# Attention's stacks turned by transposing DMAs on SP's queue instead of on TensorE

## The chip, the cores and the metric

The kernel runs on one NeuronCore of a Trainium2 chip. The metric is the time on the device of one execution, in microseconds (us). Engines are called PE (TensorE, matrix products; PEld is its weight load), DVE (VectorE), ACT (ScalarE), POOL (GpSimd) and SP (SyncE, which here only issues DMAs). SPq is SP's issuing of DMAs, as the trace shows it.

## What is computed

Two layers over 64 sequences of 64 tokens with 128 channels. Layer 0 is attention with 16 heads of 8 channels over the sequence's own keys and 64 context keys, then a feed-forward block with 8 routed experts and a shared one; layer 1 mixes a de-pooled context into the tokens and adds a two-of-eight expert block. The change touches only layer 0's attention:

```python
qkv = (x @ w_qkv.T).reshape(B, N, 3, H, D)
k = concatenate([extra_k, k]);  v = concatenate([extra_v, v])
attn = softmax(einsum('bhnd,bhmd->bhnm', q * scale, k))
out = einsum('bhnm,bhmd->bhnd', attn, v)
x = x + tanh(g_xattn[0]) * (out @ w_proj.T + b_proj)
```

## The kernel before, in words

The 4096 tokens are 32 tiles of 128 (two sequences each). The attention stage is a software pipeline over tiles that every engine walks by itself: in step k an engine does, in a fixed order written out by hand in its `step`, one piece for tile k, another for tile k-1, and so on; `stage(n)` is the tile n steps back (None outside 0 to 31). Each engine executes strictly in its written order, and semaphores (`S["name"]`) tie the engines together. `walk` peels the first steps and runs the rest in a hardware loop of four steps a turn. The stage ends at about 235 us of the profile; sorting, the routed experts and layer 1 follow and aren't touched.

For one tile t the pieces that matter are:

- ACT, stage 0 (`ctx_hi`, L678) writes the high half of the context keys into `stack[:, t%2, 2]`. PE, stage 1, makes q, k and v (L1492); ACT (L726) writes the fp16 high halves of q and k, each twice, into `stack[:, t%2, 0:2]` and signals `hi_ready`; it then saves v (L728); DVE writes the low halves (L992, `lo_ready`, and L1004 for the context keys, `ctx_stacked`). The stack has two buffers, by the tile's parity. Each of its three parts is 128 tokens x 16 heads x 32 fp16.
- PE, stage 2 (`turn_stack`, L1411) turns the three parts, four 128x128 transposes each, into PSUM banks 5 and 6: first q and k (8 transposes), later in the step the context keys (4). ACT copies the turned q to `qc` (L711), DVE the turned own keys to `ktp` (L974), ACT the turned context keys to `ktp` (L718). `qc` and `ktp` have four slots, by t%4.
- PE, stage 3 (`scores_for_max`, L1313, in two halves) computes scores from `qc` and `ktp`, and DVE takes their negative maxima (L935, four a tile). PE, stage 4, turns these (L1432), and ACT copies them to `mT` (L701, `max_kept`).
- SP, stage 3 in its own count, waits for `max_kept` and issues four small DMAs (L427, 1 KB each) that put the maxima into spare rows of `qc`; they signal `shift_placed`.
- PE, stage 5 (`scores_by_key`, L1329, two halves) waits for `shift_placed`, computes the shifted scores; ACT exponentiates them (L685); PE averages the values (`average`, L1342); then come the turn back (L1510), normalising, projection, the residual and the router's work (L1452).

SP's own step in this stage holds nothing but the wait for `max_kept` and the four DMAs. POOL spreads v, does small vector work and, from 107 us on, scatters rows to HBM (L551, indirect DMAs).

Of the kernel before, what the change touches and what calls it, by code (L numbers as in the profile page):

```python
# [102 lines left out]
def flamingo_gated_two_layers(nc, x, ctx_k, ctx_v_swapped, consts, gates, w_qkv, w_proj, b_proj, gate_w,  # L103
                              sh_gate_up, sh_down, rt_gate_up, rt_down, patch_mask, w_in, b_in, g_res, g_init,
                              router_w, router_b, expert_w, expert_b, out):
    NT = x.shape[1] // P
    D = P
    H, HD = 16, 8
# [15 lines left out]
    with ExitStack() as ctx:  # L124
# [179 lines left out]
        def by_seq(bank):  # L304
            return bank.rearrange("p (g b t) -> p b g t", g=G, b=2)

        def bank16(b):
            return PS[:, b, :].bitcast(F16)


        TILE_CHUNKS = [(0, 2), (2, 8), (8, NT)]
        x_in = [sem(f"x_in{c}") for c in range(3)]
        ck_in = [sem(f"ck_in{c}") for c in range(3)]
        cv_in = [sem(f"cv_in{c}") for c in range(3)]
        consts_in = sem("consts_in")
        weights_in = sem("weights_in")
        qkv_in, qkv_ready = sem("qkv_in"), sem("qkv_ready")
# [9 lines left out]
                 "o_kept o_turned recip_ready o_normed on_turned on_kept projected x_updated")  # L327
        S = {n: sem("a_" + n) for n in names.split()}
        shift_placed = [sem("a_shift_placed0"), sem("a_shift_placed1")]

        for n in "stats moments var_eps copied normed kept xnT_done xnT_kept routed".split():
            S["r_" + n] = sem("r_" + n)
# [44 lines left out]
        def arrived(eng, sems, tile):  # L377

            if tile is not None and tile.turn is None:
                for c, (lo, _) in enumerate(TILE_CHUNKS):  # L380
                    if tile.n == lo:
                        eng.wait_ge(sems[c], 16)
                        eng.nop(nofuse=True)

        def zero_tails(eng, half):
# [15 lines left out]
        @block.sync  # L401
        def _(sp):
            sp.dma_start(X[:, 0:2 * D], x[:, 0:2 * D]).then_inc(x_in[0], 16)
            sp.dma_start(cst[:], consts).then_inc(consts_in, 16)
            sp.dma_start(wqkv[:], w_qkv).then_inc(qkv_in, 16)
            sp.dma_start(CK[:, 0:2 * D], ctx_k[:, 0:2 * D]).then_inc(ck_in[0], 16)
            sp.dma_start(gate[:], gates).then_inc(gate_in, 16)
            sp.dma_start(wproj[:], w_proj).then_inc(weights_in, 16)
            sp.dma_start(bproj[:], b_proj).then_inc(weights_in, 16)
            sp.dma_start(gatew[:], gate_w).then_inc(weights_in, 16)  # L410
            sp.dma_start(pm_i[:], patch_mask).then_inc(mask_in, 16)
            for c in range(3):
                lo, hi = TILE_CHUNKS[c]
                if c:
                    sp.dma_start(X[:, lo * D:hi * D], x[:, lo * D:hi * D]).then_inc(x_in[c], 16)
                    sp.dma_start(CK[:, lo * D:hi * D], ctx_k[:, lo * D:hi * D]).then_inc(ck_in[c], 16)
                sp.dma_start(CV[:, lo * D:hi * D], ctx_v_swapped[:, lo * D:hi * D]).then_inc(cv_in[c], 16)
            for dst, src in ((shgu, sh_gate_up),):
                sp.dma_start(dst[:], src).then_inc(more_in, 16)

            def step(stage):
                a = stage(3)
                if a:

                    sp.wait_ge(S["max_kept"], a.done())
                    for hg in range(HG):
                        sp.dma_start(qc[32 * hg + 24:32 * hg + 25, a.slot, :, :],  # L427
                                     mT[HG * hg:HG * hg + G, a.par, :]).then_inc(shift_placed[a.par], 16)

            walk(sp, NT, LAGS, step)  # L430
            zero_tails(sp, 0)
            sp.wait_ge(rows_known, 1)
            sp.wait_ge(spare_zero, 16)
            sp.wait_ge(tails_zero, 16 * E)
            sp.wait_ge(scattered, 16 * NT)

            def load_rows(stage):
                l = stage(0)
                if l:
                    if not (l.turn is None and l.n < 4):  # L440
                        sp.wait_ge(S["e_turned"], l.freed(back=4))
                    row = sp.value_load(rows_of[0:1, ds(l.t, 1)], min_val=0, max_val=ROWS - P)
                    sp.dma_start(xs[:, l.slot, :], sorted_x[ds(row, P)]).then_inc(xs_in[l.slot], 16)

            walk(sp, NS, 2, load_rows)

            def store_out(stage):
                o = stage(12)
                if o:
                    sp.wait_ge(S["l_out_ready"], o.done())  # L450
                    sp.dma_start(out[:, o.cols(D)], X[:, o.cols(D)]).then_inc(out_done, 16)

            walk(sp, NT, 12, store_out)
            sp.wait_ge(out_done, 16 * NT)
# [210 lines left out]
        def _(act):  # L665
# [8 lines left out]

            def ctx_hi(f):
                arrived(act, ck_in, f)
                act.wait_ge(S["ctx_turned"], f.freed())
                nc.scalar.copy(parts(f.par, 2, 8, 0, 16).rearrange("p h (c d) -> p h c d", c=2),  # L678
                               twice_over(CK[:, f.cols(D)].rearrange("p (h d) -> p h d", h=H)))\
                    .then_inc(S["ctx_hi"], 1)  # L680
# [6 lines left out]
            def step(stage):  # L687
# [17 lines left out]
                if f:  # L705
                    act.wait_ge(S["qkv_done"], f.freed())
                    act.wait_ge(S["xnT_done"], f.done())
                    nc.scalar.copy(xnT[:, f.par, :], PS[:, 4, 0:P]).then_inc(S["xnT_kept"], 1)  # L708
                if s:
                    act.wait_ge(S["qk_turned"], s.done())  # L710
                    nc.scalar.copy(qc[:, s.slot], bank16(5)[:, 0:512].rearrange("p (g t) -> p g t", g=G))\  # L711
                        .then_inc(S["q_kept"], 1)
                if b:
                    exp_chunk(b, 2)
                    exp_chunk(b, 3)
                if s:
                    act.wait_ge(S["ctx_turned"], s.done())
                    last = nc.scalar.copy(ctx_half(s.slot), by_seq(bank16(6)[:, 0:512]))  # L718
                    last.then_inc(S["ctx_kept"], 1)
                if f:  # L720
                    act.wait_ge(S["qk_turned"], f.freed())
                    act.wait_ge(S["qkv_done"], f.done())

                    hi = parts(f.par, 0, 0, 8, 16).rearrange("p w h (c d) -> p w h c d", c=2)
                    qk = PS[:, 4, P:3 * P].rearrange("p (w h d) -> p w h d", w=2, h=H)
                    last = nc.scalar.copy(hi, qk.unsqueeze(3).to_broadcast([P, 2, H, 2, HD]))  # L726
                    last.then_inc(S["hi_ready"], 1)
                    nc.scalar.copy(XN2[:, ds(f.t, 1), 0:D], PS[:, 4, 3 * P:4 * P].unsqueeze(1)).then_inc(S["v_kept"], 1)  # L728
# [48 lines left out]
                    shared_gate(3, 0)  # L777
                    shared_gate(3, 1)

            walk(act, NT, 12, step, lambda: act.wait_ge(ck_in[2], 16), drain=gates_in_drain)  # L780
            act.wait_ge(S["h_acted"], Tile(EARLY - 1).done(2, 1))

            def sorted_step(stage):
# [74 lines left out]
        def _(dve):  # L858
# [79 lines left out]
            def step(stage):  # L938
# [28 lines left out]
                if m:  # L967
# [1 line left out]
                    dve.wait_ge(S["r_stats"], m.done())  # L969
                    dve.nop(nofuse=True)  # L970
                    dve.bn_aggr(mv2[:, m.par, :], str_[:, m.par, :]).then_inc(S["r_moments"], 1)  # L971
                if s:
                    dve.wait_ge(S["q_kept"], s.done())
                    last = dve.tensor_copy(own_half(s.slot), by_seq(bank16(5)[:, 512:1024]))  # L974
                    last.then_inc(S["k_kept"], 1)
# [63 lines left out]
                elif k == 12:  # L1039
                    shared_product(1, 1)  # L1040

            walk(dve, NT, 13, step, lambda: dve.wait_ge(x_in[2], 16), drain=products_in_drain)

            chained = [0]

# [246 lines left out]
        def _(pe):  # L1292
# [8 lines left out]

            def scores_for_max(a, half):

                if half == 0:
                    pe.wait_ge(S["q_kept"], a.done())
                    pe.wait_ge(S["k_kept"], a.done())
                    pe.wait_ge(S["ctx_kept"], a.done())
                pe.wait_ge(S["maxed"], a.freed(4, 2 * half + 1, back=2))
                for g in range(G):
                    for b in range(2):  # L1310
# [106 lines left out]
            def step(stage):  # L1417
# [2 lines left out]
                if a:  # L1420
                    scores_for_max(a, 0)

                if a:
                    pe.wait_ge(S["ctx_kept"], a.done())
                if rk:
                    pe.wait_ge(S["r_xnT_kept"], rk.done())
# [6 lines left out]
                                        ident16[:]).then_inc(S["max_turned"], 1)  # L1433
                if b:
                    scores_by_key(b, 0)
                if s:

                    if s.turn is None and s.n == 0:
                        pe.wait_ge(weights_ready, 1)
                    pe.wait_ge(S["hi_ready"], s.done())  # L1440
                    pe.wait_ge(S["lo_ready"], s.done())
                    turn_stack(s, 0, 5, 0, None)
                    turn_stack(s, 1, 5, 512, "qk_turned")
# [53 lines left out]
                    pe.wait_ge(S["k_placed"], ro.quad_done(2, 0))  # L1497
                if m:
                    pe.wait_ge(S["x_updated"], m.done())
                if s:  # L1500
                    pe.wait_ge(S["ctx_stacked"], s.done())
                    turn_stack(s, 2, 6, 0, "ctx_turned")
                if b:
                    average(b, 1)
                if n:
                    pe.wait_ge(S["o_kept"], n.done())
                    if s:
                        pe.wait_ge(S["k_kept"], s.done())
                    for g in range(G):
                        last = nc.tensor.transpose(PS[:, 5, g * P:g * P + P], oS[:, n.par, g * P:g * P + P], identf)  # L1510
                    last.then_inc(S["o_turned"], 1)
                if s:
                    pe.wait_ge(S["ctx_kept"], s.done())
                if rt:
                    pe.wait_ge(S["r_normed"], rt.done())
# [209 lines left out]
```

## Time and profile before

| | |
|---|---|
| median of 3 runs | 506.03 us |
| lowest and highest | 502.38 and 506.38 us |
| the profiled execution's own time | 496.49 us |
| its span in the profile | 494.9 us |
| PE, DVE, ACT, POOL busy | 445.5, 373.7, 288.3, 321.0 us |
| mean granted TensorE clock | 0.983 of full |

The profile is of one execution. A busy share says how long an engine's instructions were in flight; matmuls overlap, so a busy PE isn't PE at its peak. A row of a timeline gives the start, the length until the group's last end, engine, line, operation, written and read tiles, and the count; in brackets, the idle time before it and what ended that. "Issue" of a DMA is the time in which the issuing engine is held; landing is later.

### The profile page before, as it was taken

To read this page: it belongs to the slowest core of one execution; us is meant where nothing else is said; L and a number is where in the kernel's file an instruction comes from. 1 tells how busy PE (TensorE), PEld (TensorE's weight loads), DVE (VectorE), ACT (ScalarE), POOL (GpSimd) and SP (SyncE) were. 2 spreads that over 40 slices of the span, in tenths; PEclk is the share of its full clock that TensorE was granted. 3 is DMA by queue.
4 is the path that set the end of the run, shared out by engine and by line. 5 is a ranking of instruction groups with operands and counts; after the bars stand their busy time and mean duration, and the time that the engine had idled before them with its cause. 6 is when DMAs were issued, how large, how long until landed. Compare 5 with 4: busy or idle time off the path is not lost. (4 is left out here: it accounts for less than half of the span.)

```text
span 494.9 us, 20976 instructions
## 1 busy us (share of the span) xinstructions
PE 445.5 (90%) x6894; PEld 351.8 (71%) x6895; DVE 373.7 (76%) x1197; ACT 288.3 (58%) x803; POOL 321.0 (65%) x783
## 2 busy tenths in 40 slices
PE   1689999999999999987987999987997799999998
PEld 0457777776767777764656988864655699898997
DVE  3577999989888888954678666644766688888984
ACT  1448999999989898875225454434233344344431
POOL 5544775567777777766743665677825888998630
PEclk9999999999999999999899999998999599999999
DMA  7930000000000000000145677741000011111001
GB/s 228 413 140 4 26 26 5 5 10 15 11 12 11 11 11 12 15 15 19 55 148 147 212 222 224 221 139 32 17 11 13 16 40 37 37 39 36 23 23 33
DMA packets 22538, 33.61 MB, mean 68 GB/s; under 512 B 5592, under 2 KB 16656, under 8 KB 21968
## 3 DMA queue, kind: packets, MB, share of 16 engines
q0 software_dynamic: 7552, 20.20, 12.9%
q1 hardware_dynamic: 14352, 12.39, 7.7%
q8 instruction: 34, 0.56, 0.5%
q10 hardware_dynamic: 576, 0.26, 0.2%
q14 instruction: 24, 0.20, 0.1%
HBM read 24.82 MB, written 7.86 MB: 66 GB/s over the span
## 5 line engine op out<-in xcount | busy, mean ns | idle before, releaser
L935 DVE TENSOR_REDUCE negm<-PS 128x4 f16<-128x512 f32 x128 | 82.0, 682 | 1.1 <-PE PS L1313 0.4
L685 ACT ACTIVATE pexp<-PS 128x512 f32<-128x512 f32 x128 | 69.4, 594 | 3.8 <-PE PS L1329 3.1
L1645 PE MATMUL PS<-w,vp 128*128 128x128 f32 x512 | 63.3, 277 | 0.0
L1645 PEld LDWEIGHTS PS<-w,vp 128*128 128x128 f32 x512 | 60.5, 194 | 0.0
L1342 PE MATMUL PS<-pexp,vp 128*32 128x64 f32 x2048 | 49.4, 226 | 0.2
L1539 PE MATMUL PS<-xsT,wst 128*128 128x128 f32 x320 | 44.5, 282 | 3.5 <-DMA wst<-in_rt_gate_up_dram 1.3
L1539 PEld LDWEIGHTS PS<-xsT,wst 128*128 128x128 f32 x320 | 38.8, 191 | 8.2 <-issue 6.8
L1342 PEld LDWEIGHTS PS<-pexp,vp 128*32 128x32 f32 x2048 | 33.7, 111 | 13.8 <-issue 8.2
L551 POOL DMA_INDIRECT sorted_x<-VALL,posu x32 | 32.9, 1027 | 14.0 <-issue 7.3
L1266 DVE TENSOR_TENSOR vp<-PS,xnT 128x1024 f32<-128x1024 f32 x32 | 38.7, 1208 | 0.8 <-PE PS L1622 0.8
L1411 PEld LDWEIGHTS PS<-ident,stack 128*128 128x128 f16 x384 | 26.2, 103 | 17.9 <-issue 12.7
L580 POOL DMA_DIRECT2D wst<-in_rt_gate_up_dram x40 | 21.5, 539 | 26.6 <-PE PS L1539 18.9
L610 POOL DMA_INDIRECT VALL<-sorted_y,places x32 | 32.4, 1014 | 7.4 <-issue 7.0
L1411 PE MATMUL PS<-ident,stack 128*128 128x128 f16 x384 | 34.8, 231 | 2.0 <-DVE stack L992 2.0
L1173 DVE TENSOR_TENSOR stack<-PS,oS 128x256 f32<-128x256 f32 x40 | 16.9, 423 | 23.8 <-ACT oS L792 23.8
L852 ACT CAST mask1T<-PS 96x128 bf16<-96x128 f16 x32 | 8.4, 261 | 44.7 <-PE PS L1654 44.3
L792 ACT ACTIVATE oS<-PS 128x256 f32<-128x256 f32 x40 | 15.3, 384 | 31.7 <-PE PS L1539 31.3
L1492 PE MATMUL PS<-wqkv,xnT 128*128 128x384 f32 x64 | 32.9, 598 | 0.9 <-ACT xnT L708 0.9
L1313 PE MATMUL PS<-ktp,qc 32*64 32x128 f16 x1024 | 28.2, 230 | 4.2 <-ACT ktp L718 2.7
L492 POOL TENSOR_TENSOR ve<-mv,epsc 128x1 f32<-128x1 f32 x32 | 6.0, 188 | 39.7 <-DVE mv L971 39.5
L1553 PE MATMUL PS<-rdn,stack 128*128 x160 | 25.4, 281 | 3.6 <-DVE stack L1173 2.8
L583 POOL DMA_DIRECT2D sorted_y<-YS x40 | 21.8, 546 | 9.7 <-DVE YS L1169 4.8
(240 smaller groups left out, 1265.4 us busy)
## 6 DMA issues: line engine op xcount, KB each, us to landing
wst<-in_rt_gate_up_dram POOLq DMA_DIRECT2D x40, 256.0 KB, 3.6
xs<-sorted_x SPq DMA_DIRECT2D x40, 64.0 KB, 2.8
sorted_y<-YS POOLq DMA_DIRECT2D x40, 64.0 KB, 3.1
qc<-mT SPq DMA_DIRECT2D x128, 1.0 KB
out_dram<-X SPq DMA_DIRECT2D x32, 64.0 KB
X<-in_x_dram SPq DMA_DIRECT2D x1, 1536.0 KB, 8.5
CK<-in_ctx_k_dram SPq DMA_DIRECT2D x1, 1536.0 KB, 11.9
CV<-in_ctx_v_swapped_dram SPq DMA_DIRECT2D x1, 1536.0 KB, 17.8
```

Of the source, the lines that this page charges most:

```text
L551: pool.indirect_dma_start(out=sorted_x, out_offset=bass.IndirectOffsetOnAxis(ap=posu[:, o.t:o.t + 1], axis=0), in_=XN2[:, o.t, :], in_offs ...
L610: pool.indirect_dma_start(out=XN2[:, t, 0:D], out_offset=None, in_=sorted_y, in_offset=bass.IndirectOffsetOnAxis(ap=places[:, t:t + 1], ax ...
L685: nc.scalar.activation(pexp[:, j, :], PS[:, 2 + j % 2, :], ACT.Exp).then_inc(S["exped"], 1)
L935: dve.tensor_reduce(negm[:, a.par, :, j], PS[:, j % 2, :].rearrange("p (g k) -> p g k", g=G), AX.X, ALU.max, negate=True).then_inc(S["maxe ...
L1266: dve.tensor_tensor(z[:, m.par], PS[:, 4:6, :].rearrange("p b (e t) -> p (b e) t", t=P), xnT4[:, m.slot, :].unsqueeze(1).to_broadcast([P, ...
L1313: last = nc.tensor.matmul(PS[64 * b:64 * b + 64, hg % 2, g * P:g * P + P], qc[rows, a.slot, g, 64 * b:64 * b + 64], kt[rows, a.slot, b, g, :],
L1342: last = nc.tensor.matmul(PS[32 * g:32 * g + 32, 7, j * P + SEQ * seq:j * P + SEQ * seq + SEQ], vp[:, b.par, seq, g * HG + j, :], pexp[:, ...
L1411: last = nc.tensor.transpose(bank16(bank)[:, col + g * P:col + (g + 1) * P], stack[:, s.par, w, g * HG:g * HG + HG, :].rearrange("p h c -> ...
L1492: nc.tensor.matmul(PS[:, 4, P:4 * P], xnT[:, f.par, :], wqkv[:], start=True, stop=True)\
L1539: last = nc.tensor.matmul(PS[:, 2 + s.par, i * P:i * P + P], wst[:, s.slot, i * P:i * P + P], xsT[:, s.par, :], start=True, stop=True)
L1553: last = nc.tensor.matmul(PS[:, 6 + b.par, 0:D], act2T[:, b.par, i * P:i * P + P], rdn[:, ds(e_down * FF + i * D, D)], start=(i == 0), sto ...
L1645: nc.tensor.matmul(PS[:, 6 + y.par, 0:D], z[:, y.par, e, :], w1[:, e * D:e * D + D], start=(e == 0), stop=False)
```

## The change

From tile 4 on, PE's twelve transposes a tile (L1411) and the three copies (L711, L974, L718) go. In their place SP issues five transposing DMAs a tile, which read the stack and write straight to `qc` and `ktp`: one for q (128 tokens, 128 KB), two for the own keys (one for each sequence, 64 KB each), and two for the context keys (64 KB each). They stand in SP's step ahead of the wait for `max_kept` and the four small DMAs. All five raise `stack_turned` of the tile's parity by 16. The first three wait for `hi_ready`, `lo_ready` and for tile t-4's last scores; the last two also for `ctx_stacked`. PE's `scores_for_max` of tile t and ACT's next writes to the stack (tile t+2) wait for all five. Two semaphores are needed, so the three loads of the last chunk of tiles (8 to 31) now share one, which is waited for in full (48). The first four tiles go as before.

```diff
+        def turned_on_pe(tile):
+            return tile.turn is None and tile.n < 4
+
+        def stack_seen(eng, tile):
+
+            eng.wait_ge(stack_turned[tile.par], 80 * (tile.pair - 1))
+
+        def stack_freed(eng, tile, name):
+
+            if tile.turn is None and tile.n < 6:
+                eng.wait_ge(S[name], tile.freed())
+            else:
+                eng.wait_ge(stack_turned[tile.par], 80 * (tile.pair - 2))
+
         def bank16(b):
...
-        x_in = [sem(f"x_in{c}") for c in range(3)]
-        ck_in = [sem(f"ck_in{c}") for c in range(3)]
-        cv_in = [sem(f"cv_in{c}") for c in range(3)]
+        rest_in = sem("rest_in")
+        x_in = [sem(f"x_in{c}") for c in range(2)] + [rest_in]
+        ck_in = [sem(f"ck_in{c}") for c in range(2)] + [rest_in]
+        cv_in = [sem(f"cv_in{c}") for c in range(2)] + [rest_in]
...
-                        eng.wait_ge(sems[c], 16)
+                        eng.wait_ge(sems[c], 16 if c < 2 else 48)
...
+            def wide(par, w, b):
+                return stack[SEQ * b:SEQ * b + SEQ, par, w, 0:H, :].rearrange("p h c -> p (h c)")
+
+            def turn_stack(s):
+                sp.wait_ge(S["hi_ready"], s.done())
+                sp.wait_ge(S["lo_ready"], s.done())
+                sp.wait_ge(S["scored_t"], s.freed(4, 3, back=16))
+                sp.nop(nofuse=True)
+                sp.dma_start_transpose(qc[:, s.slot], stack[:, s.par, 0, 0:H, :].rearrange("p h c -> p (h c)"))\
+                    .then_inc(stack_turned[s.par], 16)
+                for b in range(2):
+                    sp.dma_start_transpose(own_half(s.slot)[:, b], wide(s.par, 1, b)).then_inc(stack_turned[s.par], 16)
+                sp.wait_ge(S["ctx_stacked"], s.done())
+                sp.nop(nofuse=True)
+                for b in range(2):
+                    sp.dma_start_transpose(ctx_half(s.slot)[:, b], wide(s.par, 2, b)).then_inc(stack_turned[s.par], 16)
+
             def step(stage):
-                a = stage(3)
+                s, a = stage(1), stage(3)
+                if s and not turned_on_pe(s):
+                    turn_stack(s)
                 if a:
 
                     sp.wait_ge(S["max_kept"], a.done())
...
-                act.wait_ge(S["ctx_turned"], f.freed())
+                stack_freed(act, f, "ctx_turned")
...
-                if s:
+                if s and turned_on_pe(s):
                     act.wait_ge(S["qk_turned"], s.done())
                     nc.scalar.copy(qc[:, s.slot], bank16(5)[:, 0:512].rearrange("p (g t) -> p g t", g=G))\
                         .then_inc(S["q_kept"], 1)
...
-                if s:
+                if s and turned_on_pe(s):
                     act.wait_ge(S["ctx_turned"], s.done())
                     last = nc.scalar.copy(ctx_half(s.slot), by_seq(bank16(6)[:, 0:512]))
                     last.then_inc(S["ctx_kept"], 1)
                 if f:
-                    act.wait_ge(S["qk_turned"], f.freed())
+                    stack_freed(act, f, "qk_turned")
                     act.wait_ge(S["qkv_done"], f.done())
 
                     hi = parts(f.par, 0, 0, 8, 16).rearrange("p w h (c d) -> p w h c d", c=2)
...
-                if s:
+                if s and turned_on_pe(s):
                     dve.wait_ge(S["q_kept"], s.done())
                     last = dve.tensor_copy(own_half(s.slot), by_seq(bank16(5)[:, 512:1024]))
                     last.then_inc(S["k_kept"], 1)
...
-                if half == 0:
+                if half == 0 and turned_on_pe(a):
                     pe.wait_ge(S["q_kept"], a.done())
                     pe.wait_ge(S["k_kept"], a.done())
                     pe.wait_ge(S["ctx_kept"], a.done())
+                elif half == 0:
+                    stack_seen(pe, a)
...
-                if a:
+                if a and turned_on_pe(a):
                     pe.wait_ge(S["ctx_kept"], a.done())
...
-                if s:
+                if s and turned_on_pe(s):
...
-                if s:
+                if s and turned_on_pe(s):
                     pe.wait_ge(S["ctx_stacked"], s.done())
                     turn_stack(s, 2, 6, 0, "ctx_turned")
...
-                    if s:
+                    if s and turned_on_pe(s):
                         pe.wait_ge(S["k_kept"], s.done())
...
```

## Rows read from the trace of the kernel before

**Rows 1.** The span in 40 slices: busy tenths, granted clock.
```profile
PE   1689999999999999987987999987997799999998
...
PEclk9999999999999999999899999998999599999999
```

**Rows 2.** Busy time of each engine in two stretches of attention.
```profile
core 0: us, PE busy (x) PEld busy (x) DVE busy (x) ACT busy (x) POOL busy (x), PEclk, DMA share, GB/s
60.00:120.00 60.00, 59.40 (x1527) 43.82 (x1523) 54.90 (x167) 55.19 (x150) 38.80 (x119) 1.00 0.04 12
120.00:180.00 60.00, 58.43 (x1479) 42.83 (x1479) 53.52 (x169) 54.17 (x146) 45.08 (x127) 1.00 0.04 12
```

**Rows 3.** Waits from 60 to 180 us: in total, times, longest.
```profile
ACT ktp L718 <- PE PS L1411: 5.6, 20, 0.4
...
PE PS L1510 <- DVE ktp L974: 1.2, 3, 0.4
```

**Rows 4.** SP's four small DMAs of one tile, and all 128 of L427.
```profile
39.68 2.42 SPq L427 DMA_DIRECT2D qc<-mT  x4
...
L427 SPq DMA_DIRECT2D qc<-mT x128: 572/573/742, 25.2 to 219.3; - x128
```

**Rows 5.** ACT in one step, in order of time.
```profile
117.76 0.25 ACT L701 COPY mT<-PS 16x128 f16<-16x128 f16 x1
...
119.18 0.59 ACT L711 COPY qc<-PS 128x512 f16<-128x512 f16 x1
...
121.15 0.58 ACT L718 COPY ktp<-PS 128x512 f16<-128x512 f16 x1 [0.26 <-PE PS L1411]
121.63 0.59 ACT L726 CAST stack<-PS 128x512 f16<-128x512 f32 x1
...
124.06 0.25 ACT L701 COPY mT<-PS 16x128 f16<-16x128 f16 x1
```

**Rows 6.** DVE in one step, in order of time.
```profile
116.80 0.41 DVE L992 TENSOR_TENSOR stack<-PS,stack 128x256 f16<-128x256 f32 x1
...
117.38 0.28 DVE L1004 TENSOR_TENSOR stack<-CK,stack 128x128 f16<-128x128 f16 x1
...
120.55 0.39 DVE L974 COPY ktp<-PS 128x512 f16<-128x512 f16 x1
...
122.60 0.41 DVE L992 TENSOR_TENSOR stack<-PS,stack 128x256 f16<-128x256 f32 x1
```

**Rows 7.** PE in one step, in order of time.
```profile
117.42 0.41 PE L1329 MATMUL PS<-qc,ktp 32*128 32x64 f16 x16
117.75 0.62 PE L1411 MATMUL PS<-ident,stack 128*128 128x128 f16 x8
118.21 0.34 PE L1452 MATMUL PS<-gatew,xrT 128*128 128x8 f32 x2
...
120.73 0.39 PE L1411 MATMUL PS<-ident,stack 128*128 128x128 f16 x4
121.04 0.43 PE L1342 MATMUL PS<-pexp,vp 128*32 128x64 f32 x16
...
123.78 0.41 PE L1329 MATMUL PS<-qc,ktp 32*128 32x64 f16 x16
```

**Rows 8.** The turns alone (L1411), 60 to 180 us.
```profile
60.00:180.00 120.00, 19.12 (x228) 14.37 (x228) 1.00 0.04 12
```

**Rows 9.** Other DMAs by line: issue ns min/median/max, landing us.
```profile
L443 SPq DMA_DIRECT2D xs<-sorted_x x40: 337/338/365, 254.2 to 321.3; - x40
...
DMA to landing us min/median/max: 1.7/2.8/4.0
...
L551 POOL DMA_INDIRECT sorted_x<-VALL,posu x32: 967/1034/1125, 107.4 to 251.2; - x32
...
L595 POOL DMA_DIRECT2D ssv<-ssv x2: 532/539/546, 327.4 to 327.9; - x2
...
DMA to landing us min/median/max: 2.1/2.2/2.3
```

**Rows 10.** Layer 1: stretches where PE waits, with the granted clock.
```profile
380.00:385.00 5.00, 3.28 (x23) 2.43 (x21) 2.09 (x9) 1.41 (x5) 3.38 (x9) 0.88 0.05 15
385.00:390.00 5.00, 2.88 (x18) 2.44 (x19) 3.49 (x17) 2.48 (x9) 4.46 (x10) 0.50 0.04 13
...
395.00:400.00 5.00, 5.00 (x57) 4.87 (x56) 4.28 (x19) 2.88 (x10) 4.49 (x10) 1.00 0.10 28
```

More of the change, by code:

```diff
@@ L329, in flamingo_gated_two_layers @@
         shift_placed = [sem("a_shift_placed0"), sem("a_shift_placed1")]
+        stack_turned = [sem("a_stack_turned0"), sem("a_stack_turned1")]
         for n in "stats moments var_eps copied normed kept xnT_done xnT_kept routed".split():
@@ L778, in gates_in_drain @@
                     shared_gate(3, 1)
-            walk(act, NT, 12, step, lambda: act.wait_ge(ck_in[2], 16), drain=gates_in_drain)
+            walk(act, NT, 12, step, lambda: act.wait_ge(rest_in, 48), drain=gates_in_drain)
             act.wait_ge(S["h_acted"], Tile(EARLY - 1).done(2, 1))
@@ L1040, in products_in_drain @@
                     shared_product(1, 1)
-            walk(dve, NT, 13, step, lambda: dve.wait_ge(x_in[2], 16), drain=products_in_drain)
+            walk(dve, NT, 13, step, lambda: dve.wait_ge(rest_in, 48), drain=products_in_drain)
             chained = [0]
@@ L1511, in step @@
                     last.then_inc(S["o_turned"], 1)
-                if s:
+                if s and turned_on_pe(s):
                     pe.wait_ge(S["ctx_kept"], s.done())
```

## The prediction, made before the changed kernel ran

> **What bounds the kernel now.** First the span in 40 slices: from the third slice on PE is at 8 or 9 tenths and its granted clock at 9 through the whole attention stage [rows 1]. Next the length of a step. SP's four small DMAs mark it once a tile: the third tile's group starts at 39.68 us, the last DMA of all 128 at 219.3, so the last group at 219.3 - 3 x 0.617 = 217.45, and (217.45 - 39.68) / 29 = 6.13 us a tile [rows 4]. (0.617 is the pitch within a group, (2.42 - 0.573) / 3.) Then what each engine does in such a step. In 60 us (9.79 tiles) PE is busy 59.40, ACT 55.19, DVE 54.90: 6.07, 5.64 and 5.61 us a tile [rows 2]. The reader is to see that three engines are nearly full at once and that the waits between 60 and 180 us are small: 5.6 us in all where ACT waits for the turned context keys, 1.2 us where PE waits for DVE's copy [rows 3]. PE, in its fixed order, sets the pace, with ACT and DVE half a microsecond behind. SP is the idle one: 4 issues, 2.47 us of every 6.13 [rows 4].
>
> **What goes.** PE's twelve turns. Busy time says 19.12 us for 228, 1.0 us a tile [rows 8], but they overlap with their neighbours; what counts is when the next group can start: 117.75 to 118.21 for the eight, 120.73 to 121.04 for the four, 0.46 + 0.31 = 0.77 us of PE's order [rows 7]. ACT loses two copies, 0.59 + 0.58 = 1.17 us [rows 5], DVE one, 0.39 us [rows 6]. Left a tile: PE about 5.3, ACT 4.5, DVE 5.2 us. If nothing else came in, the step would be some 5.4 us, 0.73 less, over 28 tiles 20 us. That is the prize.
>
> **What comes.** Five transposing DMAs a tile on SP, ahead of the four small ones in its order. No row shows a transposing DMA. Issue of one on SP: the cheapest DMA of SP's queue is 0.338 us (plain rows, 64 KB), the small scattered ones take 0.573 [rows 4, 9]; POOL's indirect DMA, whose addresses are made row by row for 128 rows, takes 1.034 [rows 9]. A transposing DMA sends each 2-byte element of a row to another partition, so its addresses are more work than those of a plain copy of rows; the nearest row is the one in which addresses cost the issuer, so I take 1.03, a guess by kinship, with 0.34 as the low end. For the high end I take the whole time from issue to landing of an SBUF to SBUF DMA, 2.2 us [rows 9], as if each held the queue until it had landed. With the 0.044 us between two issues (0.617 - 0.573) one is 1.08 us, five are 5.39, and with the four small ones SP needs 5.39 + 2.47 = 7.86 us a tile. SP can't hide that: it does it for every one of the tiles 4 to 31, and everything in the stage needs what it issues.
>
> The Trainium skill has a price of its own: "DMA: Bandwidth & Descriptors", section "Why a DMA increments its semaphore by 16 and not by 1", gives for generations before the newest 512 sequencer cycles for a plain DMA, 631 for a small transposing one and, from SBUF to SBUF, 32 cycles for each piece (262,144 for 8,192). Scaled by this trace's 0.43 us plain loads that is an estimate of 5.2 us for the five (96 pieces of 16 rows by 128 columns), so nearly the sum above; no row here shows it.
>
> **The waits.** Queued behind SP's wait for `hi_ready` and `lo_ready` are the four small DMAs of tile t-2, which used to go as soon as `max_kept` came. The low halves are done at 116.80 + 0.41 = 117.21, the maxima are copied at 118.01 [rows 5, 6]. Before, the four go out from 118.03; now five issues stand between, and SP comes to them at 117.21 + 5.39 = 122.6, is through at 125.1, and they land 2.2 us after the last issue began, 126.7. PE needs them for the keyed scores at 123.78 [rows 7]: about 3 us late. Behind PE's wait for them its whole step is queued. That closes a loop over two steps: low halves done, nine issues, landing, keyed scores, and PE's and DVE's way to the next low halves. The last piece is 117.42 to 123.01, 5.59, less the 0.77 of turns, 4.82 [rows 6, 7]. In all (5.39 + 2.47 - 0.62 + 2.2 + 4.82) / 2 = 7.1 us a tile. SP's own 7.86 is above that, so the queue's throughput decides and the loop fits inside. `scores_for_max` and ACT's next stack write need the five landed; they are looser by the small DMAs' 2.47 us. The wait for tile t-4's last scores is met a step earlier. The merged load semaphore is needed at tile 8, about 60 us, when the loads (traffic before 35 us) are long in: nothing. The transfers themselves: 384 KB a tile beside a DMA share of 0.04 [rows 2]. A plain 64 KB lands 2.8 us after its issue began, 4.0 at most [rows 9], and the five overlap one another and the issues; inside 7.9 us I take them as hidden.
>
> **The sum.** 7.86 - 6.13 = 1.73 us a tile, 28 tiles: 48.4 us. The first such tile finds SP idle and pays nothing for the first half microsecond; I call the whole 48. The gain on PE, ACT and DVE (20 us alone) is swallowed, since all three then wait for SP. On the profiled execution's 496.49 us that gives 544.5. The median of the runs lies 9.5 us above that execution, and the shown runs differ from it by 6 to 10 us without the profile saying where, so I add the loss to the median: 506 + 48 = 554 us. With the price between 0.85 and 1.3 us an issue the likeliest case's own range is 528 to 592.
>
> **Rivals.**
> - *The issue is as cheap as a plain DMA's (28%).* For it: SP's other issues are all 0.34 to 0.57 [rows 4, 9]. Against: none of them is cut in so many pieces. The loop then decides, with pitch x: (5x + 2.47 - 0.62 + 2.2 + 4.82) / 2. At 0.382 it is 5.39 us, 28 x -0.74 = -21, 485 us; at 0.617 it is 5.98, -4, 502 us. Middle 493. It breaks even at x = 0.68, an issue of 0.63 us. This is the other sign: below 0.63 us an issue the change isn't slower, above about 0.7 it is. I give 20% to faster by over 1% and 8% to within 1%. In "Advanced Engine Details and Errata", section "X-Bar Transpose (TRN2)", the Trainium skill says that transposing DMAs are as fast as regular ones; by that rule it is this case's upper point, 502.
> - *Each transposing DMA holds the queue until it lands (8%).* Five x 2.2 + 2.47 = 13.5 us a tile, 28 x 7.3 = 206, 712 us. For it: no row excludes that one must be done before the next begins. Against: the four small DMAs go out every 0.617 us [rows 4], far faster than anything lands.
> - *The clock falls (10%).* PE would wait some 2.5 us of every 7.9. In layer 1, where it waits like this, its clock is granted at 0.88 and 0.50 in two stretches with 3.28 and 2.88 us busy of 5, and 1.00 where it is full [rows 10]. At 0.5 (the 1.2 of its two levels, 1.2 and 2.4 GHz) PE's 5.3 us grow toward 8, and as the chain passes PE I put the step at 9.0: 28 x 2.9 = 80, 586 us.
> - *Everything is hidden and nothing gained (2%):* within 1% of 506.
>
> **How the numbers follow.** 52% for 554; 28, 8, 10 and 2% for the others. Slower by over 1% is 52 + 8 + 10 = 70%, within 1% (about what a measurement of this kernel can tell from no change) 8 + 2 = 10%, faster 20%. The range leaves out the lower half of the cheap case and the serial case with the dearest end of mine: 494 to 612.
>
> **What would show it.** Right: SP's five issues of about 1 us each, its queue without a gap from tile 4 on; a pitch of 7.9 us between groups of small DMAs; PE, ACT and DVE each waiting 2 us or more a step, PE at L1329's keyed scores for `qc<-mT`; the stage ending near 280 us and all behind it as before. Wrong: an issue below 0.63 us (then PE waits little and the step is under 6.13), small DMAs landing late though SP has gaps (then the transfers or their flow bind, not the issue), or L1411's absence leaving PE as full as now.

## The result, and the profile after

The changed kernel takes 603.19 us (median of 5 runs, 601.95 to 608.08), the kernel before 502.38 us beside it (median of 5, 500.58 to 506.38): ratio 1.206, 95% interval 1.200 to 1.212. By the two medians it is 101 us slower, where the prediction reckoned 48. The profiled execution took 608.08 us, its span 606.5. Here and below, ratios leave out single executions that ran more than 1.5% above the fastest of their kernel.

First the slices (the page of the kernel after; answers to [rows 1]):

```profile
PE   2787878788879977799879797999789969999998
...
PEclk9995676667676677865655998999969998999999
```

PE's clock, which stood at full speed through the stage before, is granted at 5 to 8 tenths from the fourth slice to the twenty-second, which is where the stage now ends, and PE is mostly at 7 or 8 tenths. Two stretches of attention say the same (answers to [rows 2], same columns):

```profile
60.00:120.00 60.00, 48.78 (x834) 30.97 (x834) 31.20 (x90) 27.86 (x76) 22.32 (x71) 0.64 0.24 47
120.00:180.00 60.00, 50.59 (x857) 32.87 (x853) 31.92 (x100) 28.44 (x77) 25.34 (x75) 0.66 0.25 46
```

DVE and ACT, nearly full before (54.90 and 55.19 of 60), are at half. So all three wait for something outside them. What that is stands in the issues of SP, by line (issue ns min/median/max, first and last start; answers to [rows 4]; under a line, who waited for it, in us and times):

```profile
L445 SPq DMA_TRANSPOSE qc<-stack x28: 1175/1198/1874, 38.4 to 302.7; - x28
L448 SPq DMA_TRANSPOSE ktp<-stack x56: 1236/1249/2199, 39.7 to 305.3; - x56
L452 SPq DMA_TRANSPOSE ktp<-stack x56: 1184/1249/2608, 43.3 to 308.8; - x56
...
  ACT stack L713: 50.0, 26
  PE PS L1350: 18.8, 13
...
L462 SPq DMA_DIRECT2D qc<-mT x128: 572/573/920, 25.2 to 322.9; - x128
...
  PE PS L1366: 24.2, 24
```

The reader is to take two numbers from it. The pitch: the queries' DMA (L445) goes once a tile, so a step is (302.7 - 38.4) / 27 = 9.79 us, against 6.13 before, and (9.79 - 6.13) x 28 = 102 us, the loss between the medians. And the price: 1.20 us for one of the queries, 1.25 for one of the keys, whereas a small plain DMA still takes 0.573. SP's queue in order of time shows that the pitch is these issues and little else:

```profile
97.61 1.20 SPq L445 DMA_TRANSPOSE qc<-stack  x1
98.85 2.54 SPq L448 DMA_TRANSPOSE ktp<-stack  x2
101.48 3.53 SPq L452 DMA_TRANSPOSE ktp<-stack  x2
105.06 2.43 SPq L462 DMA_DIRECT2D qc<-mT  x4
108.24 1.20 SPq L445 DMA_TRANSPOSE qc<-stack  x1
```

Each is followed by the next; from the first of these DMAs to the last no gap in the queue is over 0.76 us. L452's two take 3.53 us here, where two at the median are 2.54: now and then one issue is stretched, up to 2.61 us. With those (15 of the 140 took 1.6 to 2.6 us) the five of a tile come to 6.63 us on average (1.25 + 2 x 1.33 + 2 x 1.36), the four small ones to 2.47, and 0.69 lies between them. Last the waits, from 60 to 240 us:

```profile
ACT stack L713 <- DMA ktp<-stack: 36.3, 18, 3.5
...
PE PS L1366 <- DMA qc<-mT: 15.6, 16, 1.4
...
PE PS L1350 <- DMA ktp<-stack: 11.2, 10, 2.3
```

All three wait for what SP issues, and none of the three was there before. L713 is ACT's write of the context keys' high halves into the stack, L1366 PE's keyed scores, L1350 its `scores_for_max`.

### The profile page after: what moved, and what is told of

Its sections match the earlier page's. It is cut to its first block and busy times, and to the rows that moved or that the text cites. A ratio compares the mean times of both kernels' runs of the same rounds, so it can differ in the third digit from the quotient of the medians.

```text
span 606.5 us, 20390 instructions
## 1 busy us (share of the span) xinstructions
PE 510.3 (84%) x6558; PEld 381.0 (63%) x6559; DVE 368.5 (61%) x1169; ACT 266.2 (44%) x747; POOL 318.8 (53%) x783
## 5 line engine op out<-in xcount | busy, mean ns | idle before, releaser
L1379 PEld LDWEIGHTS PS<-pexp,vp 128*32 128x32 f32 x2048 | 46.5, 145 | 47.1 <-issue 40.7
L1379 PE MATMUL PS<-pexp,vp 128*32 128x64 f32 x2048 | 67.2, 283 | 0.7 <-ACT pexp L720 0.4
L1366 PE MATMUL PS<-qc,ktp 32*128 32x64 f16 x1024 | 34.5, 220 | 24.5 <-DMA qc<-mT 24.2
L1350 PE MATMUL PS<-ktp,qc 32*64 32x128 f16 x1024 | 35.3, 274 | 22.4 <-DMA ktp<-stack 18.8
L1529 PE MATMUL PS<-wqkv,xnT 128*128 128x384 f32 x64 | 49.8, 879 | 0.9 <-ACT xnT L743 0.9
L1366 PEld LDWEIGHTS PS<-qc,ktp 32*128 32x128 f16 x1024 | 25.1, 111 | 34.3 <-DMA qc<-mT 23.3
L1350 PEld LDWEIGHTS PS<-ktp,qc 32*64 32x64 f16 x1024 | 22.1, 134 | 30.9 <-DMA ktp<-stack 12.0
L984 DVE TENSOR_TENSOR X<-PS,X 128x128 f32<-128x128 f32 (+1 forms) x32 | 9.3, 292 | 51.3 <-PE PS L1512 51.3
L1018 DVE RECIPROCAL rden<-PS 128x16 f32<-128x16 f32 x32 | 8.2, 258 | 49.9 <-PE PS L1547 49.8
L713 ACT CAST stack<-CK 128x256 f16 (+1 forms) x32 | 13.0, 408 | 50.0 <-DMA ktp<-stack 50.0
L1547 PE MATMUL PS<-cst,oS 128*128 128x128 f32 x128 | 33.3, 411 | 0.5 <-DVE X L984 0.5
```

The source lines that it names most:

```text
L1350: last = nc.tensor.matmul(PS[64 * b:64 * b + 64, hg % 2, g * P:g * P + P], qc[rows, a.slot, g, 64 * b:64 * b + 64], kt[rows, a.slot, b, g, :],
L1366: last = nc.tensor.matmul(PS[:, 2 + hg % 2, at:at + SEQ], kt[rows, b.slot, seq, g, :], qc[rows, b.slot, g, SEQ * seq:SEQ * seq + SEQ], sta ...
L1379: last = nc.tensor.matmul(PS[32 * g:32 * g + 32, 7, j * P + SEQ * seq:j * P + SEQ * seq + SEQ], vp[:, b.par, seq, g * HG + j, :], pexp[:, ...
L1529: nc.tensor.matmul(PS[:, 4, P:4 * P], xnT[:, f.par, :], wqkv[:], start=True, stop=True)\
```

## The experiments

Theory A: SP's queue sets the step, by its number of DMAs. Rivals: B, the price goes by pieces or rows, or the landing binds; C, PE's clock, which falls because PE waits, makes the loss. Six of the runs hold the clock by idle products, which nothing reads, at the places where PE would wait (the form with a choice of columns; the three earlier runs take 512):

```
def fill(bank, n, cols):
    pe.wait_ge(more_in, 16)
    for i in range(n):
        nc.tensor.matmul(PS[:, bank, 0:cols], identf, shgu[:, 0:cols], start=True, stop=True)
```

All ratios are to runs of the kernel before on the same chip, with their 95% interval. That kernel itself had medians from 501 to 515 us on the chips used, so times are compared as ratios, and steps by the pitch between SP's DMAs.

**Nothing removed, the DMAs alone added,** into a tile that nothing reads (against the changed kernel):

```
-   if s and turned_on_pe(s):
+   if s:
...
        turn_stack(s, 1, 5, 512, "qk_turned")
...
-   sp.dma_start_transpose(own_half(s.slot)[:, b], ...)
+   sp.dma_start_transpose(scr(s.par, 1, b), ...)
```

> PE, ACT and DVE turn the stacks as before, and the five transposing DMAs are issued as well, into a tile that nothing reads; the stacks are freed when they have landed. Queue theory: the same step as after's, 9.7 us, and a ratio of 1.17 to 1.20, though nothing was taken from PE, ACT or DVE. Had the loss come from a clock that fell because PE had less to do, or from PE's wait for keys that land late, the ratio would be below 1.10.

608.7 us, ratio 1.213 (1.204 to 1.223).

```profile
L449 SPq DMA_TRANSPOSE scratch<-stack x28: 1197/1200/1952, 38.4 to 308.3; - x28
```

(308.3 - 38.4) / 27 = 10.0 us a step. The loss is all there though nothing was taken from the three engines and no key waits for a transfer. ACT's next write to the stack still waits for the landing here, so this run alone doesn't tell the queue from that wait; the next two, which change the number of DMAs at the same bytes, do. The work taken from the engines bought at most the 0.2 us between 10.0 and 9.79.

**Six and three DMAs.** The queries' one 128x512 DMA as two of 64 rows; or the own and the context keys by one DMA of 128 rows each (three in all; the keys of the two sequences then land in another order, so that run's output isn't the reference's).

```
-   sp.dma_start_transpose(qc[:, s.slot], stack[...])
+   for b in range(2):
+       sp.dma_start_transpose(qc[:, s.slot, :, SEQ * b:SEQ * b + SEQ], wide(s.par, 0, b))
...
-   for b in range(2):
-       sp.dma_start_transpose(own_half(s.slot)[:, b], wide(s.par, 1, b))
+   sp.dma_start_transpose(ktp[:, s.slot, 0:4 * P].rearrange("p (g t) -> p g t", g=G), stack[...])
```

> The changed kernel with q turned by two DMAs of 64 rows instead of one of 128: the same bytes and pieces in six DMAs a tile. Theory A with a price for each DMA of about 1.25 us whatever its rows: the step grows by 1.25 + 0.04, 28 x 1.29 = 36 us more, about 639 us. If the price goes by the pieces that a DMA moves: under 8 us more. Rival C: about half of A, 18 us more.

640.94 us, ratio 1.245 (1.235 to 1.255); the changed kernel run again on a third chip had 602.52 and 1.177 (1.165 to 1.189).

```profile
L446 SPq DMA_TRANSPOSE qc<-stack x56: 711/1240/1548, 38.4 to 336.6; - x56
```

Half the rows cost 1.24 us where all of them cost 1.20. The price is one per DMA, not per row or piece. The step is (336.6 - 1.24 - 38.4) / 27 = 11.0 us (336.6 is the second of a pair): one DMA more is 1.2 us a tile, 34 us over 28 tiles.

> The changed kernel unaltered, beside the others on one chip, since the kernel before took 502 us on the first chip and 515 on the second. If SP's queue sets the step whatever the chip, about 603 us again; if the clock has a part in it, 610 us or more on a chip that grants the kernel before less clock.

> The changed kernel with the own and the context keys turned by one DMA of 128 rows each instead of two of 64: three DMAs a tile with the same bytes, the keys of the two sequences landing in another order, so its output isn't the reference's. Queue theory with a price for each DMA: SP needs 9.79 - 2 x 1.35 = 7.1 us, 28 x 2.7 = 75 us less, about 528 us. With the clock still halving in the waits, PE's own step (9.6 us where its clock is at half, about 5.6 at full) takes the place of SP's: 545 us or more. If the price goes by pieces: about 603 us, no gain.

562.31 us, ratio 1.097 (1.084 to 1.110), 8.42 us a step: far better than five, but above the 7.1 of its queue, with a mean clock of 0.863. So a second term comes up once the queue is shorter. With three short idle products:

> The three transposing DMAs of three_dmas (its values are rearranged as there) with three idle products of 128 columns, some 0.6 us a tile, where PE waits for the keys and for the shifts. Queue and clock theory: SP's step of three issues and the four small DMAs is 7.0 to 7.2 us, so at a full clock the time is some 530 to 535 us against three_dmas' 562, ratio near 1.04. If the clock is not held, the ratio stays near 1.10. If landing, not issue, were the limit, the step would be above 8 us at a full clock too.

530.39 us, ratio 1.054 (1.043 to 1.065).

```profile
L445 SPq DMA_TRANSPOSE qc<-stack x28: 1197/1200/1681, 38.4 to 235.2; - x28
```

7.29 us a step, and from 147 us on, where the clock was whole, steps of 6.6 to 7.0: the queue's 3.68 (its three medians) + 2.47 and half a microsecond of gaps. With larger products (some 2.95 us a tile: 1.03 for one, 1.92 for two in a row) PE itself became the bound, busy 59.07 of the 60 us from 60 us on:

> The three-DMA variant with idle products in PE's waits (two of 512 columns ahead of the small DMAs' wait, one ahead of the turned stack's; same misplaced keys). If the clock took part of the gain of the three-DMA variant, this one is faster than it by 10 us or more at a clock over 0.95, near 528 us. If the queue alone counts, the same time within 1%.

571.54 us, ratio 1.117, at a clock of 0.958: a miss as an experiment, since the fill was longer than the wait.

**The clock under the changed kernel.** Four idle products of 512 columns a tile:

> The changed kernel with idle products on PE (two of 512 columns with the identity, into banks about to be overwritten) ahead of each of its two waits for SP's DMAs, so that PE is busy where it waited. Theory A: the granted clock rises over 0.9 in the attention stage and the time stays within 1% of 603 us. Rival B (the clock costs part of the step): the time falls by 20 us or more. If the fillers themselves delay PE, it rises by up to 28 x 1.8 = 50 us.

602.56 us, ratio 1.170 (1.161 to 1.180), against the unfilled kernel's 1.177 on another chip.

```profile
60.00:120.00 60.00, 55.48 (x864) 29.79 (x858) 31.87 (x89) 26.95 (x75) 22.43 (x71) 0.97 0.24 47
...
L445 SPq DMA_TRANSPOSE qc<-stack x28: 1197/1198/1905, 38.2 to 300.9; - x28
```

The clock is back at 0.97 and the pitch is (300.9 - 38.2) / 27 = 9.73, the same. Theory C falls for this kernel. One reservation: a pair of products turned out at 1.98 us, so PE was busy 55.48 of 60 us, 9.0 us in a step of 9.7, and could nearly have set the step itself. What speaks against that is SP's queue, which had no gap over 0.75 us here either.

**The prize alone.** No turns on PE, no copies of them and no transposing DMAs from the fifth tile on, so that the scores are made of the first four tiles' stacks:

```
     def turn_stack(s):
-        sp.wait_ge(S["hi_ready"], s.done())
...
+        pass
```

> The changed kernel with no turn at all from tile 4 on: neither PE nor SP turns the stacks, and the scores of tiles 4 to 31 are computed from the first four tiles' turned q and keys, so its output isn't the reference's. It shows the prize. My prediction's account: a step of 5.4 us against 6.13, about 20 us less than the kernel before, some 482 us. Rival: other chains (the maxima's way over SP, DVE's order) hold the step above 5.9, and the gain is under 7 us.

533.27 us, ratio 1.036 (1.028 to 1.044), mean clock 0.901. Slower than before, with the work simply gone. Two stretches of it:

```profile
160.00:165.00 5.00, 5.00 (x79) 2.99 (x75) 2.17 (x8) 2.23 (x7) 3.85 (x12) 0.50 0.00 1
...
175.00:180.00 5.00, 4.56 (x98) 2.95 (x102) 3.59 (x11) 4.32 (x12) 4.48 (x13) 1.00 0.04 14
```

At a full clock most of its steps are 5.7 us, where the kernel before has 6.1 in the same stretch (76 to 93 us) and 5.4 was reckoned; but from about 100 us on the clock drops to half in stretches, and a step that lies mostly in one takes 8.5 to 9.4. A few such eat the gain of all the others. Two fills:

> The variant without any turn (533 us on the second chip, its clock at 1.0 or 0.5 by stretches, output not the reference's) with one idle product of 512 columns a tile on PE ahead of its wait for the small DMAs. If the lost prize is the clock (PE, freed of its turns, waits a little and its clock is halved), the clock stays over 0.97 and the time falls to about 490 to 500 us, though PE does more. Rival (another chain binds without the turns): it stays at 533 or rises.

527.57 us, ratio 1.029 (1.018 to 1.040), clock 0.971: one product of 512 columns, some 1.0 us of PE's order, is more than the 0.77 of the turns.

> No turning at all from the fifth tile on, as in no_turns (the scores are then made of stale stacks), with one idle product of 128 columns, some 0.2 us, ahead of PE's wait for the shifts of each of those tiles. If no_turns was slower than before by the clock alone, the clock stays near 1.0 here, the step is some 5.8 us and the time 10 us under before's. If the missing work itself gives nothing, the time is before's or more at a full clock. If so short a product doesn't hold the clock, it stays near 0.90 and the time near no_turns' ratio of 1.04.

505.82 us, ratio 1.007 (1.002 to 1.011); the profiled execution is the slowest of nine (513.07 us, clock 0.946), those compared had 0.959 to 0.969. Its steps were mostly 6.0 to 6.1 us at a full clock, not 5.8: the idle product takes 0.42 us of the order of a PE that is 49.06 of 50 us busy (70 to 120 us), about what the missing turns gave, and the clock still dropped in two places of the stage. No run showed the twenty microseconds. The fills show that the clock follows what PE does; why it dropped here, where PE waited so little, no run shows.

**Room in SP's queue.** The four small DMAs on POOL:

```
-   sp.dma_start(qc[32 * hg + 24:32 * hg + 25, a.slot, :, :], mT[...])
+   pool.dma_start(qc[32 * hg + 24:32 * hg + 25, a.slot, :, :], mT[...])
```

> The changed kernel with the four small DMAs of each tile issued by POOL instead of SP. Theory A (SP's queue is the bound: every issue held there adds its length to the step): the step falls from 9.79 us by 2.47 to about 7.3, 28 x 2.47 = 69 us less, about 534 us. Rival B (the fallen TensorE clock sets the step): no more than 10 us gained. Rival C (the latency loop over two steps binds, not the queue's throughput): half of A, about 568 us.

580.39 us, ratio 1.127 (1.118 to 1.137), 8.82 us a step where SP's issues fill 6.8. SP now waits 1.8 to 4.6 us at 16 places, about every second tile. With the clock filled:

> The changed kernel with the four small DMAs on POOL's queue, as small_on_pool, and with three idle products of 256 columns, some 1.3 us a tile, at PE's two waits. The five transposing DMAs alone take 6.6 us a tile. If the clock at half ate what the queue gave back, the clock is above 0.95, the step 7 to 7.6 us and the time 530 to 545 against small_on_pool's ratio of 1.127. If the path from the scores through the shifts on POOL and the next stacks to SP's queue is what sets it, the step stays at 8.5 us or more at a full clock and the ratio near 1.12.

567.22 us (558.74 to 581.48, against 506.15 for the kernel before), too uneven for a ratio; the profiled execution is the slowest of the three. Its early part has half-clock stretches; from 200 to 260 us the clock is whole and the steps are 7.5 to 8.6. Both of the expectation's answers held in part: the clock ate some, and even at a full one the step was longer than the queue's 6.8, though the fill itself, 1.3 us by the expectation, lies on PE's way. The second bound is best seen in the kernel in which the four small DMAs are one:

```
-   for hg in range(HG):
-       sp.dma_start(qc[32 * hg + 24:32 * hg + 25, a.slot, :, :], mT[HG * hg:HG * hg + G, a.par, :])
+   sp.dma_start(qc[24:P:32, a.slot, :, :], mT[:, a.par, :])
```

> The changed kernel with the four small DMAs of a tile as one DMA of 16 rows. Queue theory: 6.6 us for the five and 0.6 for the one, with 0.4 of gaps 7.6 us a tile: 1.5 x 28 = 41 us over before, 548 us, if the clock is held, and up to 575 where it isn't (as in three_dmas, which stood at 8.4 for a queue of 7.1). If the cost of a small DMA goes by the rows that it moves, it takes as long as the four did and the time is after's 603.

573.1 us, ratio 1.135 (1.127 to 1.144), 8.77 us a step; the one DMA of 16 rows takes 0.533 us, no longer than each of the four. In this run the trace also has the landing of the transposing DMAs:

```profile
L448 SPq DMA_TRANSPOSE ktp<-stack x56: 1231/1247/2353, 39.6 to 277.6; - x56
...
DMA to landing us min/median/max: 2.4/2.4/4.4
```

Two steps of its timeline, SP, PE and DVE:

```profile
137.62 0.41 DVE L1025 TENSOR_TENSOR stack<-PS,stack 128x256 f16<-128x256 f32 x1
...
138.27 1.20 SPq L445 DMA_TRANSPOSE qc<-stack  x1
139.52 3.19 SPq L448 DMA_TRANSPOSE ktp<-stack  x2
...
142.80 3.51 SPq L452 DMA_TRANSPOSE ktp<-stack  x2
...
147.59 0.64 PE L1348 MATMUL PS<-ktp,qc 32*64 32x128 f16 x16 [4.10 <-DMA ktp<-stack]
...
152.70 1.65 PE L1527 MATMUL PS<-wqkv,xnT 128*128 128x384 f32 x2
...
153.73 0.53 SPq L461 DMA_DIRECT2D qc<-mT  x1
...
156.53 0.41 DVE L1025 TENSOR_TENSOR stack<-PS,stack 128x256 f16<-128x256 f32 x1
...
157.28 1.23 SPq L445 DMA_TRANSPOSE qc<-stack  x1
```

This is the loop over two steps. The low halves of one tile are done at 138.03; SP's five issues run to 146.31; `scores_for_max` (L1348), which waited 4.10 us for them to land, begins at 147.59; PE's way from there ends in the low halves of the tile after next at 156.94, and SP, idle since 154.26, takes them at 157.28. That is 19.0 us for two steps. How long PE's part is hangs on the clock (same kernel):

```profile
138.00:147.00 9.00, 5.25 (x138) 3.49 (x126) 5.96 (x19) 3.94 (x10) 6.32 (x17) 1.00 0.37 55
148.00:157.00 9.00, 8.80 (x138) 5.70 (x126) 5.31 (x18) 5.08 (x15) 3.66 (x12) 0.50 0.24 46
```

Here it is 9.35 us at a clock of 0.50; in the run with the small DMAs on POOL the same way took 6.0 us at a full clock (82.36 to 88.40). PE waits at a full clock and works at half.

**What can be kept.** Only the queries' stack turned by a DMA, the two key stacks by PE:

```
     sp.dma_start_transpose(qc[:, s.slot], stack[...]).then_inc(stack_turned[s.par], 16)
-    for b in range(2):
-        sp.dma_start_transpose(own_half(s.slot)[:, b], wide(s.par, 1, b)).then_inc(stack_turned[s.par], 16)
...
-    if s and turned_on_pe(s):
+    if s:
         pe.wait_ge(S["ctx_stacked"], s.done())
         turn_stack(s, 2, 6, 0, "ctx_turned")
```

> Only the queries' stack is turned by a DMA, one of 128x512 a tile; PE turns the keys' and the context's as before. SP has 1.25 + 2.47 + 0.4 = 4.1 us a tile, under the step, PE loses 0.3 us and ACT a copy of about 0.4 us. Queue theory: the loss goes altogether, the step is 5.9 to 6.1 us and the time 496 to 506 against before's 506, with the clock at 0.95 or more. Rival, a clock that falls as in no_turns: ratio 1.01 to 1.04 with a mean clock near 0.9. Rival, a DMA whose latency is late on the path: step above 6.5 us at a full clock.

497.99 us, ratio 0.994 (0.989 to 0.998), step 6.1 us as before, clock 0.979. The loss goes. With one small DMA in place of four, before and here:

> The kernel before with the four small DMAs of a tile as one of 16 rows. SP's queue is idle for 3.7 us a tile there, so the count of its DMAs sets nothing: within 1% of before. If the shifts come late on the path (four issues in a row are 2.4 us behind the copy of the maxima), the time falls by up to 5 us, which is then no gain of the turned stacks in q_own_one_small.

> The same kernel as before_one_small, in five rounds. If its 1% is real, the ratio is 0.985 to 0.995 again. Its step in the trace was 6.17 us against before's 6.18, so the gain should not be there by the step, and the theory that SP's count sets nothing where its queue is idle expects 1.00.

Ratio 0.990 (0.982 to 0.997) in the first run, 1.000 (0.996 to 1.004) in the second with 12 executions against 23: nothing. The first interval, from three executions, did not hold up.

> q_alone with one small DMA of 16 rows in place of four. SP has 1.25 + 0.6 us a tile. If the gains of q_alone and of the merged DMA are real and add, the ratio is 0.98 to 0.99. If both are noise of the clock, it is 1.00 within half a per cent. Rival: the clock falls as in q_own_one_small, mean below 0.96 and ratio above 1.00.

499.0 us, ratio 0.997 (0.992 to 1.001). So neither gain is established; no version here beats the kernel before by what can be told apart. And with the own keys on SP too:

> Queries and own keys turned by three DMAs, the context's keys by PE as before, and one small DMA of 16 rows. SP has 3 x 1.3 + 0.6 + 0.4 = 4.9 us a tile, under the step; PE loses 8 of 12 turns, 0.5 us, ACT and DVE a copy each. Queue theory: not slower than before at a full clock, step 5.8 to 6.0, 495 to 502 where before has 501 to 506; ratio 0.98 to 1.00. Rival, the clock: with 0.5 us less work PE waits more, and as in no_turns the mean falls to 0.9 or so, ratio 1.02 to 1.05.

519.9 us, ratio 1.028 (1.022 to 1.035), though SP's queue has room (1.19 + 2 x 1.25 + 0.53 = 4.2 us of issues at their medians, in a step of 6.95). Its mean clock was 0.940.

```profile
105.00:110.00 5.00, 5.00 (x69) 3.25 (x69) 2.07 (x6) 2.63 (x6) 3.20 (x11) 0.50 0.12 23
...
115.00:120.00 5.00, 4.75 (x124) 3.38 (x124) 4.40 (x12) 4.43 (x13) 4.47 (x13) 1.00 0.24 43
```

Most of its steps are 5.8 to 6.4 us at a full clock and 7.5 to 11.3 with half-clock stretches in them: by its trace the rival of that expectation, the clock, came true. The same kernel with the clock held was not run.

## Why the prediction came out as it did

- *What bounds the kernel before, and the pace of PE:* right in kind. At a full clock, without turns, the step is 5.7 us for the 5.4 reckoned, 0.4 less than the 6.1 beside it and not 0.73.
- *"SP's queue without a gap", its throughput sets the step, not the work removed:* right, and shown by the run with the DMAs alone (10.0 us a step with nothing removed), the filled one (9.73) and the step that follows the number of DMAs at the same bytes (11.0 and 9.79 us for six and five, 7.29 for three with short idle products).
- *The price, "I take 1.03, a guess by kinship":* this is the term that failed. The five take 6.20 us at their medians, not 5.17, which is 1.03 x 28 = 29 us; stretched issues bring 0.43 more, 12 us. The gaps outside the small group were reckoned at 5 x 0.044 = 0.22 us a tile and came to 0.69, 13 us. Together 54 us, and 48 + 54 = 102. The wide end of the likeliest case, 1.3 us an issue, had the median in it but neither the stretches nor the gaps. What makes an issue stretch, and what fills the gaps, was not found. The two profiled executions lie 111.6 us apart; 106.8 are there at the next stage's first load (254.2 and 361.0 us), the rest comes behind the stage, which the prediction took as unchanged.
- *The order of the price, by pieces, in the sentence from the Trainium skill ("DMA: Bandwidth & Descriptors", section "Why a DMA increments its semaphore by 16 and not by 1"):* the dependence on pieces isn't borne out here. 128 rows cost 1.20 to 1.27 us and 64 rows 1.24 to 1.25. The estimate by it, 5.2 us, was short of the 6.20 by the same microsecond as the prediction's own.
- *The loop over two steps, "7.1 us a tile" and inside the queue's time:* inside, yes; its size was wrong where it came to matter. By the prediction's own formula with 6.63 us for the five and its 0.22 of gaps it would be 7.9 us at a full clock for the changed kernel (worked out, not measured), and PE's part is 3 us longer at half clock (9.35 for 6.0). Its path was not quite the one named either: the prediction closed it at the keyed scores and called `scores_for_max` and ACT's stack writes looser. In the changed kernel PE waited at both (24.2 us in all at the keyed scores, 18.8 at `scores_for_max`) and ACT 50.0 us at the stack, and where the small DMAs are off the queue or one, the loop closes at `scores_for_max`. That is why each relief of the queue gave less than reckoned (8.8 us a step with small DMAs on POOL or merged, in place of 6.8 to 7.6).
- *Rival, cheap issue (28%):* wrong; the cheapest of the 140 is 1.18 us. The Trainium skill's rule beside it, that transposing is as fast as a regular DMA ("Advanced Engine Details and Errata", section "X-Bar Transpose (TRN2)"), doesn't hold for the issue, 1.25 against 0.573 us. For the time to landing the traces don't speak against it: in the run with one small DMA the transposing ones of 64 KB landed 2.4 us after their issue began (median), a plain load of 64 KB in 2.8 [rows 9].
- *Rival, serial until landing (8%):* wrong. The issues follow each other at 1.2 to 1.3 us.
- *Rival, the clock falls (10%), 586 us:* it fell, to 0.64, as described. It is nearer to 603 than the forecast, but not the reason: with the clock held the time is the same.
- *"The prize", 20 us:* wrong, without consequence for the forecast. The prediction took PE's busy time less the turns at an unchanged clock. The run without any turning was 3.6% slower than before, at a mean clock of 0.901.
- *What would show it:* the pitch was 9.79 us, not 7.9; the stage's last small DMA went at 322.9 us, 103.6 later than before, so it ended near 335 and not near 280; PE waited at the keyed scores as named, but not 2 us a step, since at half clock it is busy instead of waiting. The transfers stayed hidden (DMA share 0.24).

## What to carry over

Price a change that moves work onto a DMA queue by the number of DMAs times the issue of that very kind, and if no row has that kind, measure one first: between 0.63 us (break-even) and 1.25 us lay the whole sign of this change. SP's queue had 3.7 us of a 6.13 us step free; three such issues (3.68) fill that, five are 6.6, and what they relieve is then worth nothing. Where TensorE is full and at its top clock, taking work from it is not a gain by itself: look for what keeps it busy afterwards.

## What the runs showed of the hardware

- A transposing DMA of fp16 from SBUF to SBUF holds SP for 1.20 to 1.27 us (128x512) or 1.24 to 1.25 us (64x512) at the median, a small plain one for 0.573, one with 16 rows for 0.533. Single issues of the transposing kind are stretched to 2.6 us (15 of 140 in the changed kernel).
- PE's clock alternated between full speed and half where PE waited for SP's DMAs in most steps (changed kernel: busy 48.78 of 60 us, clock 0.64; with idle products: 55.48 of 60, clock 0.97). It also dropped where eight or all twelve turns were gone and SP had room (no turns: mean 0.90, for 0.97 of the kernel before on that chip; queries and own keys by DMA: 0.94), and not in the one with the queries alone by DMA (0.979; the kernel before 0.983 in its profile).
- A step of this stage that lies mostly at half clock takes 8.5 to 10 us for 5.7 to 6.1, though only PE is slowed (DVE's L1025 takes 0.41 us in either stretch), since every other engine hangs on it.
